# A cross-attention encoder layer: z and q through DRAM, half of relu by DVE alone, three low parts on POOL, all orders written anew

## The reference, cut to what matters

```
q = x @ Wq + bq ; k = c @ Wk + bk ; v = c @ Wv + bv        # per head of 16
scores = q . k / 4 ; only keys j < i are allowed ; row 0 of attn set to 0
attn = softmax(scores) ; ctx = attn @ v
z   = layer_norm(x + ctx @ Wo + bo, g1, b1n)
out = layer_norm(z + relu(z @ W1 + b1) @ W2 + b2, g2, b2n)
```

## Time and profile before

| | |
|---|---|
| time, three runs | 1668.69 us median (1667.07 to 1668.77) |
| the profiled execution | 1669.3 us, its span 1667.4 us |
| busy, PE / ACT / DVE / POOL | 97% / 93% / 86% / 83% of the span |
| HBM | 104.73 MB read, 50.33 MB written |
| mean granted TensorE clock | 0.983 of full speed; 1.00 between 100 and 1600 us |

### The profile page before, as it was taken

One profiled execution on the slowest core, in us unless ns is written; L12 is line 12 of the kernel. 1 busy time (PEld: TensorE's weight loads), 2 busy tenths in 40 slices (PEclk: granted clock), 3 DMA queues, 4 the chain that ended last, 5 costly groups with the idle time before them and its releaser, 6 DMA issues.

```text
span 1667.4 us, 54091 instructions
## 1 busy us (share of the span) xinstructions
PE 1619.5 (97%) x16700; PEld 1592.4 (95%) x16700; DVE 1432.2 (86%) x6735; ACT 1549.0 (93%) x5907; POOL 1386.5 (83%) x1358
## 2 busy tenths in 40 slices
PE   4799999999999999999999999999999999999997
PEld 3699999999999999999999999999999999999996
DVE  3688898898898898898898898898898889889874
ACT  3799999999999999999999999999999999999993
POOL 2368888888888888888888888888888888888896
PEclk7799999999999999999999999999999999999999
DMA  7856656656666655665665665665665665665520
GB/s 146 174 118 123 131 134 121 131 126 127 133 135 116 135 133 117 136 134 120 132 137 117 132 134 121 135 131 126 127 134 126 128 130 128 127 130 130 112 60 27
DMA packets 307071, 208.99 MB, mean 125 GB/s; under 512 B 164320, under 2 KB 281952, under 8 KB 306784
## 3 DMA queue, kind: packets, MB, share of 16 engines
q1 hardware_dynamic: 305088, 204.60, 59.6%
q10 hardware_dynamic: 1696, 0.92, 0.3%
HBM read 104.73 MB, written 50.33 MB: 93 GB/s over the span
## 4 chain that ended last, share of the span: by engine, by line
PE 94%; DMA 1%; SPq 1%; DVE 1%; ACT 1%; issue 1%; POOL 1%; POOLq 0%; ACTq 0%; DVEq 0%
PE ps_dense L377 32%; PE ps_dense L387 32%; PE ps_probsT L480 14%; PE ps_scores L470 7%; PE ps_att L498 7%; PE ps_dense L359 2%; ACT probs L575 0%; DMA k_spill<-kT 0%; SPq L278 0%; DMA k_stack<-k_spill 0%; POOL hT L1014 0%; DMA probs<-in_L_xattn_Wk_dram 0%; SPq L235 0%; DMA q_stack<-qT 0%; SPq L241 0%
## 5 line engine op out<-in xcount | busy, mean ns | idle before, releaser
L575 ACT ACTIVATE probs<-ps_scores,negmax 128x128 f32<-128x128 f32 x2048 | 744.2, 413 | 8.4 <-DVE negmax L782 5.0
L1006 POOL TENSOR_TENSOR probs<-probs,recip 128x512 f32<-128x512 f32 x512 | 534.2, 1044 | 136.7 <-DVE recip L765 136.5
L782 DVE CUSTOM_DVE_ANT_0 ps_scores<-ps_scores,mask 128x128 f32<-128x128 f32 x2048 | 527.6, 319 | 71.8 <-PE ps_scores L470 69.6
L575 ACT ACTIVATION_READ_ACCUMULATOR probs<-ps_scores,negmax 128x1 f32 x2048 | 517.4, 253 | 0.0
L387 PE MATMUL ps_dense<-w,hT 128*128 128x256 f32 x3072 | 420.9, 286 | 1.8 <-DVE u L903 0.9
L377 PE MATMUL ps_dense<-zT,w 128*128 128x256 f32 x3072 | 416.9, 285 | 0.5 <-DVE h_f L866 0.5
L1014 POOL TENSOR_TENSOR hT<-h_f,hT 128x512 fp32r<-128x512 f32 x256 | 327.6, 1294 | 93.3 <-DVE h_f L866 93.3
L377 PEld LDWEIGHTS ps_dense<-zT,w 128*128 128x128 f32 x3072 | 381.8, 189 | 0.9 <-issue 0.9
L387 PEld LDWEIGHTS ps_dense<-w,hT 128*128 128x128 f32 x3072 | 380.3, 188 | 2.3 <-issue 1.2
L592 ACT ACTIVATE probsT<-ps_probsT 128x508 f32<-128x508 f32 x512 | 319.2, 623 | 40.3 <-PE ps_probsT L480 40.1
L480 PE MATMUL ps_probsT<-ident,probs 128*128 128x128 f32 x2048 | 314.9, 276 | 0.0
(11 more groups left out here) (84 smaller groups left out, 2335.3 us busy)
## 6 DMA issues: line engine op xcount, KB each, us to landing
k_stack<-k_spill SPq DMA_DIRECT2D x384, 128.0 KB, 4.4
q_stack<-qT SPq DMA_DIRECT2D x762, 64.0 KB, 2.0
k_spill<-kT SPq DMA_DIRECT2D x128, 256.0 KB, 2.2
c_tok<-in_ctx_dram SPq DMA_DIRECT2D x256, 64.0 KB, 4.8
x_res<-in_x_dram SPq DMA_DIRECT2D x64, 256.0 KB, 3.1
out_dram<-o_tok SPq DMA_DIRECT2D x64, 256.0 KB, 2.8
x_tok<-in_x_dram SPq DMA_DIRECT2D x252, 64.0 KB, 2.4
probsT<-in_L_xattn_W_dram SPq DMA_DIRECT2D x1, 1024.0 KB, 11.1
```

The source lines that it names most:

```text
L575: last = nc.scalar.activation(probs[:, m % 4, i, :], ps_scores[m % 2][:, i, :], ACT.Exp, bias=negmax[:, m % 4, i:i + 1], scale=-1.0, accum ...
L782: last = nc.vector.tensor_tensor_reduce(ps_scores[m % 2][:, i, :], ps_scores[m % 2][:, i, :], mask[:], -1.0, -MASKED, ALU.add, ALU.min, ac ...
L1006: nc.gpsimd.tensor_tensor(probs[:, m % 4], probs[:, m % 4], recip[:, m % 4, :].unsqueeze(2).broadcast_to([P, 4, S]), ALU.mult)\
```

## The change

- **z through DRAM.** The transposes on PE go, and with them one product in the PSUM banks. SP writes z of a group to DRAM (`spill_z`), reads it back in 32x32 blocks (`load_z`) into the buffer of the residual (`x_res`), DVE turns it in place (`z_flips`), ACT rounds (`z_hi`), POOL subtracts (`z_lo`). The load of the next residual waits for that (`load_residual` now needs `s_zlo`). W1 is loaded with its rows in the matching order.
- **q through DRAM.** Two spills and three loads in place of twelve DMAs from SBUF to SBUF.
- **Two of four parts of relu.** relu(u + b1) = max(u, -b1) + b1. For the parts 1 and 3, DVE writes the high part of max(u, -b1) and then the low part, both from PSUM (`h_shifted`, four instructions of 256 columns). ACT and POOL have nothing to do with these parts. What is left out, b1 @ W2 over these parts, is made once (`fold_shift`, four matmuls) and added to the row that the second normalisation adds anyway (`fold_rows`).
- **The low parts of x, c and z** are subtracted by POOL.
- **Orders anew.** All five lists, the bank table, and how far apart the steps of a group stand: `ff_up(3)` and all four `ff_down` of a group are now one iteration after its `ff_up(0)` to `ff_up(2)`.

```diff
-BANK = {"zT": 2, "v": 0, "q": 2, "f1_0": 2, "k": 0, "f1_1": 1, "f1_2": 2, "f1_3": 0, "wo": 1, "f2": 1}
+BANK = {"v": 0, "q": 2, "f1_0": 1, "k": 1, "f1_1": 0, "f1_2": 1, "f1_3": 2, "wo": 2, "f2": 0}
...
+            def spill_z(g):
+                    sp.wait_ge(s_z1, GB * (g + 1))
+                    sp.dma_start(z_dram[g % 2].rearrange("b s d -> s b d"), u1[:]).then_inc(s_zspill, 16)
+            def load_z(g):
+                    sp.wait_ge(s_zspill, 16 * (g + 1))
+                    sp.wait_ge(taken["wo"], g + 1)
+                    for j in range(4):
+                        sp.dma_start(z_tile[32 * j:32 * j + 32], z_blocks[g % 2, j]).then_inc(s_zrow, 16)
...
             def load_residual(g):
-                    need(sp, taken["wo"], g)
+                    need(sp, s_zlo, g)
                     sp.dma_start(x_res[:], x_v[g]).then_inc(s_xres, 16)
...
-            def z_transpose(g):
-                if exists(g):
-                    pe.wait_ge(s_z1, GB * (g + 1))
-                    transposes(g, "zT", u1)
...
+            def h_shifted(g, n):
+                    dve.wait_ge(full[f"f1_{n}"], g + 1)
+                    for i in range(2):
+                        nc.vector.tensor_scalar(hT[:, 0, ch, :], ps_dense[BANK[f"f1_{n}"]][:, i * GT:(i + 1) * GT],
+                                                neg_b1[:, ch:ch + 1], None, ALU.max).then_inc(s_hshift, 1)
+                    for i in range(2):
+                        dve.wait_ge(s_hshift, done + i + 1)
+                        last = nc.vector.scalar_tensor_tensor(
+                            out=hT[:, 1, ch, :], in0=ps_dense[BANK[f"f1_{n}"]][:, i * GT:(i + 1) * GT],
+                            scalar=neg_b1[:, ch:ch + 1], in1=f32(hT[:, 0, ch, :]), op0=ALU.max, op1=ALU.subtract)
...
+            def z_lo(g):
+                    pool.wait_ge(s_hi["zT"], g + 1)
+                    nc.gpsimd.tensor_tensor(zT[:, 1].rearrange("p c (o t) -> p c o t", t=32), z_by_chunk(),
+                                            f32(zT[:, 0]).rearrange("p c (o t) -> p c o t", t=32), ALU.subtract)\
+                      .then_inc(s_zlo, 1)
```

More of the change, by code:

```diff
@@ L175, in encoder_layer @@
         s_att_lo = sem("att_taken")
-        s_hlo = [sem(f"h{n}_lo") for n in range(4)]
+        s_hlo = {n: sem(f"h{n}_lo") for n in (0, 2)}
         s_st1 = sem("stats1_ready")
@@ L197, in f32, with z_by_chunk @@
             return ap.bitcast(F32)
+        z_tile = x_res[:].rearrange("p b d -> p (b d)").rearrange("p (o k) -> p o k", k=KC * 32)
+        def z_by_chunk():
+            return z_tile.rearrange("p o (c t) -> p c o t", c=KC)
+        q_by_pair = q_stack[0][:].rearrange("p (c j) t -> p j c t", j=4)
+        SHIFTED_CHUNKS = [2 * n + i for n in SHIFTED for i in range(2)]
+        b1_wide = h_f32[:, 1].rearrange("p c (i t) -> p (c i) t", i=2)
         WEIGHTS = [(Wq, wq, KC, D), (Wk, wk, KC, D), (Wv, wv, KC, D), (Wo, wo, KC, D), (W1, w1, KC, FF),
@@ L325, in _ @@
             load_x(2)
-            stack_q(0, 1, True)
+            stack_q0(2)
+            stack_q0(3)
             load_c(2)
@@ L353, in bank_free @@
                     pe.wait_ge(taken[prev], (g + 1) * TAKES.get(prev, 1))
[L355 to L362, removed]
             def weights_split(g, n):
@@ L615, in z_hi @@
                 if exists(g):
-                    take_hi("zT", zT, g, full["f1_3"], g)
+                    act.wait_ge(s_zflip, g + 1)
+                    need(act, full["f1_3"], g)
+                    nc.scalar.activation(zT[:, 0].rearrange("p c (o t) -> p c o t", t=32), z_by_chunk(), ACT.Copy)\
+                      .then_inc(s_hi["zT"], 1)
             def projection_hi(g, name, dst, bias):
@@ L642, in q_hi @@
                 if exists(g) and (g > 0 or first):
-                    for i in range(2):
-                        need(act, s_qstack[i], 16 * 2 * PARTS * g)
+                    if g == 1:
+                        act.wait_ge(s_qfirst, 16 * 4 * PARTS)
+                    for part in range(2):
+                        need(act, s_qspill[part], 16 * (g - 1))
                     projection_hi(g, "q", qT, bq_col)
@@ L714, in iteration @@
                 exponentials(it + 1, 1)
-                h_hi(it - 1, 0)
+                k_hi(it + 2)
                 take_probsT(it, 6)
                 exponentials(it + 1, 2)
+                q_hi(it + 3)
+                norm2(it - 3)
+                take_probsT(it, 7)
             first_loads()
@@ L900, in norm1_sum @@
                     dve.wait_ge(s_xb, g + 1)
-                    need(dve, full["zT"], g)
+                    need(dve, s_zspill, 16 * g)
                     need(dve, s_zg, g)
```

319 lines of the change are left out of this document (190 added, 129 removed).

## The result

The changed kernel is slower: 1716.9 us median of four runs (1714.8 to 1724.5) against 1668.7 (1667.1 to 1669.4), ratio 1.030 with a 95% interval of 1.027 to 1.033. I had predicted 1644, faster. The profiled execution took 1714.8 us, its span 1713.0.

A forecast was written before the change was run, and what follows sets the result against it. PE was taken to bound the kernel, busy all of each 24.87 us period. From 1669.3: -27.5 + 2 - 2 + 1 - 4 + 6 = 1644.8, so 1644 us by the median; forecast 1638 to 1652, range 1637 to 1668.

The forecast's parts named there:

- period with nothing waited for: Time per group in mid-program, set by PE: from 24.87 us down to 24.43 without z's transposes.
- waits in mid-program: PE's loss to tight loops between groups: 0.03 us per group, +2 us in all.
- start: First groups: -2 for SP's prologue and earlier k, +1 for fold_shift, -4 for group 2's iteration.
- end: Last group: three rows come back and z waits for its DRAM trip, net +6 us.
- It fits, with 0 to 1.4 us to spare: Each iteration: k_stack lands 23.0 to 24.4 us after the first scores; the next scores want it at 24.43.
- The loop: First scores, ACT, POOL's z_lo, SP's loads of residual, x and k_stack, next first scores; called the tightest.
- Rival 1: The loop through the residual and k_stack decides: 0.15 to 0.3 us more in 62 groups, 1654 to 1664; chance 0.23.
- z at 0.43 us a group: On PE, z's transposes cost 0.43 us per group; removing them saves 27.5 us over 64 groups.
- Another order could change what follows what by some hundredths; I take none: PE's new instruction order: changed neighbours were given no cost, everything else on PE staying the same.
- the -4 for group 2's iteration: In the start, three rows of 12 stand one iteration later, leaving PE less to do: -4 us (0 to -6).
- Rival 3: POOL becomes the bound in mid-program and the kernel slower, 1686 us at a period of 25.1; chance 0.15.
- the argument "against": On POOL: h_lo stood late behind its relu, so in the new order its largest wait has no reason left.

The follow-up runs named there:

- e10: The changed kernel with z read back into a buffer of its own, so the residual's load no longer waits for z_lo; 1672.9 us, ratio 1.0028.
- e3: The kernel before with only one of z's four transposes per group, so z is wrong; 1648.6 us, ratio 0.988.
- e9: e8 with the transposes of unit 3 ahead of ff_up(2) on PE, so that v_project follows a row of 12; 1715.5 us, ratio 1.028.
- e6: The changed kernel with x's loads behind k_stack and PE's attend ahead of the transposes of unit 0; 1705.2 us, ratio 1.021.
- e8: The changed kernel with x's loads behind k_stack, SP's start reordered (group 1's q and k earlier) and attend behind the fifth scores; 1717.2 us, ratio 1.030.
- e2: The changed kernel with q of group 1 spilled ahead of the rows and loaded ahead of W1 in SP's start; 1715.1 us, ratio 1.028.
- e11: e10 with e8's start in SP's list and fold_shift one unit later; 1667.4 us, ratio 0.9991 to the kernel before.
- e7: The changed kernel with q neither spilled nor loaded from group 2 on, so the output is wrong; 1719.1 us, ratio 1.030.
- e1: The changed kernel with the residual's load behind k_stack, one iteration later in SP's list; 1911.6 us, ratio 1.144.

## Why the prediction was wrong

| term | predicted | measured |
|---|---|---|
| period with nothing waited for | 24.43 | 24.586 (e10, mean of 60; 24.61 in mid-program), so -15.5 over 60 groups and not 60 x 0.43 = -25.8 |
| waits in mid-program | +2 | +42.1 (25.287 against e10's 24.586, 60 groups) |
| start | -5 | +11.0 |
| end | +6 | +8.0 |

The measured terms make the 45.6 us of span.

- **"It fits, with 0 to 1.4 us to spare": the step that failed.** The loop was the right one, and x_res went out when I said. I closed it with a landing of 4.4, the median of 384 loads, where scores wait for the last of six: a median of 5.8 us from its issue to the scores where PE waited. In some iterations the issues were long too, x's four 3.68 us in the one shown for my 2.1 to 2.68; the median start of the last issue, 19.95, was still inside my 18.6 to 20.0. And a loop whose slack is 0 at one end of its own range was given the price of its good end (0.03 us a group). Rival 1 was the right mechanism; its price, 0.15 to 0.3 a group, was again by the median. It measured 0.70, 42 us. PE's timeline shows 30.3 of them as waits, in the 43 iterations from 120.20 on that end in one (the wait that ends at 120.20 belongs to the start). These iterations are together 10.0 us longer than their waits and 24.61 explain, and the 16 others 1.7 us. About 0.16 us each of that is how a wait is counted: from the end of v's row as the profile models it (1.65 us), where without a wait the scores start 1.49 us into the row.
- **z at 0.43 us a group: right** (e3, three quarters of it). ACT need not have been relieved for it: at 97% it let PE go at full pace there.
- **"Another order could change what follows what by some hundredths; I take none": the second step that failed, by 0.17 us a group, 10 us.** The hundredths came, on many rows. By the starts of PE's groups in one iteration of each trace (from 805.44 before, from 807.18 in e10), the twelve rows take 17.87 us in e10 and took 17.63 before: the row ahead of attention takes 1.61 us (814.58 to 816.19 in the changed kernel) where others behind transposes take 1.49 to 1.52, and v took 1.49 where it had 1.37. How much each neighbour is worth alone stays open: e9 moved v and gained nothing, e6 and e8 moved attention and met waits.
- **The start.** The first scores of group 2 came at 95.36, 13.5 us later than before, where I had -1. Of the -4 for group 2's iteration 2.5 came (27.3 to 24.8, 1.9 of it a wait as in mid-program). What failed is the SP prologue: I asked when k is there, and not what q's spill, at its end, holds back. It is not that spill alone, since moving it gave nothing (e2). e10 to e11 brings the first scores of group 3 from 118.10 to 112.40, by SP's order and fold_shift's place together.
- **The end** was within 2 us. PE waits 2.2 us for z_lo of the last group, and 1.0 and 1.9 us at rows of ff_down with no releaser named.
- **Rival 3 did not come.** POOL is at 88%. Its sum (22.4 of a period) was right, 362.93 of 400 us or 22.3 of 24.61 in e10, and its waits shrank as the argument "against" said. var_eps takes a median of 0.20 us between 120 and 1600 us, but up to 1.27; what the long ones cost, no run here shows. **DMA load** at 0.79 was as predicted, and harmless (e7).

## What to carry to other kernels

Close a loop through waits with the slowest issue and landing that the trace shows for its DMAs, not with the median; where the slack comes out as "0 to something", the loop decides, and its price belongs in the forecast. A buffer that two transfers share adds a wait to an ordered DMA list: ask what stands behind it there, and test by giving it a buffer of its own. An instruction between two units of a two-bank ring is the ring's time; moving it by one place can cost more than the edit it is to mend.

## What the runs showed of the hardware

- **Landing time depends on the place in the queue.** A 256 KB load of x_res took a median of 3.0 us from issue to landing in the changed kernel, and 6.71 in the iteration of e1 shown, behind six loads of k_stack. k_spill took 2.2 us before, 4.8 right behind q_stack's three loads of 256 KB, and 2.2 again with q's transfers gone (e7). The page "DMA: Bandwidth & Descriptors" of the Trainium skill (section "Queues, rings and completion order") says that each DMA engine consumes a ring's descriptors in order, and that a completion lands only behind the earlier writes of that engine. The traces agree in this: a transfer with more bytes just ahead of it in the queue lands later. They don't show single descriptors.
- **PE in mid-program can wait for 2% of the time at full clock** (1.00 in the window of the changed kernel, PE busy 390.55 of 400). In e1, busy 363 of 400, it was 0.98.
- **A row of 12 matmuls has a length by its neighbours** (from its start to the next start, in the kernel before and in e10): 1.36 to 1.44 us behind another row or behind scores, 1.46 to 1.52 behind transposes, 1.61 behind transposes and ahead of attention. Scores ahead of attention took 0.33 us where others take 0.24.
